# Gated cross-attention with a routed feed-forward layer: four row buffers, W_qv loaded earlier, high halves of the first rows first, the last tile in column halves, and 36 matmuls that nobody reads

## The reference

```
x   = x + tanh(g_xattn) * xattn(layernorm(x), ctx)      # x: 4096 x 512, ctx: 3202 x 512
        Sim     = softmax over ctx of a trilinear similarity;  hq_hat = softmax(Sim) @ ctx
        hc_bar  = softmax(rowmax(Sim)) @ hc               # one row for all
        feats   = [hc, hq_hat, hc * hq_hat, hc * hc_bar];  feats @ W_qv + b_qv      # W_qv: 2048 x 512
x   = x + tanh(g_ffn) * ffn(layernorm(x))
        gates = softmax(x @ w_router);  top 2 of 8 experts, at most 640 rows for each
        h = gelu(rows @ w1[e] + b1[e]);  out = h @ w2[e] + b2[e];  weighted sum for each token
```

## Time and profile before

| | us |
|---|---|
| median of 3 runs | 2236.64 (2236.12 to 2238.46) |
| the profiled execution, its own time | 2254.05 |
| its span, first to last instruction | 2252.3 |
| PE busy in the span | 2172.4 (96%) |
| DVE busy | 1301.3 (58%) |
| ACT busy | 1142.2 (51%) |
| GpSimd busy | 145.7 (6%) |
| mean granted TensorE clock | 0.989 of full speed |

### The profile page before, as it was taken

One profiled execution on the slowest core, in us unless ns is written; L12 is line 12 of the kernel. 1 busy time (PEld: TensorE's weight loads), 2 busy tenths in 40 slices (PEclk: granted clock), 3 DMA queues, 4 the chain that ended last, 5 costly groups with the idle time before them and its releaser, 6 DMA issues.

```text
span 2252.3 us, 34528 instructions
## 1 busy us (share of the span) xinstructions
PE 2172.4 (96%) x12015; PEld 1123.7 (50%) x12015; DVE 1301.3 (58%) x2712; ACT 1142.2 (51%) x1747; POOL 145.7 (6%) x141
## 2 busy tenths in 40 slices
PE   5999999999999999999999995999999999999997
PEld 2444444444444444444455442646565565647463
DVE  7756566655555665554667665555556464646450
ACT  6765565655555655655433342625354363636260
POOL 0000000000000000000022222010101010010101
PEclk9999999999999999999999997999999999999999
DMA  9534444444444444335987762353433333343511
GB/s 250 133 86 94 111 110 104 106 111 93 92 108 109 111 97 115 87 84 120 269 232 206 186 160 50 144 128 100 103 102 98 107 93 107 93 116 117 132 35 23
DMA packets 484566, 265.91 MB, mean 118 GB/s; under 512 B 423860, under 2 KB 423988, under 8 KB 480428
## 3 DMA queue, kind: packets, MB, share of 16 engines
q1 hardware_dynamic: 473644, 244.90, 41.6%
q0 software_dynamic: 10880, 20.52, 4.8%
HBM read 97.96 MB, written 71.52 MB: 75 GB/s over the span
## 4 chain that ended last, share of the span: by engine, by line
PE 88%; DMA 4%; DVE 4%; issue 2%; ACT 1%; POOL 1%; SPq 0%; POOLq 0%; DVEq 0%; ACTq 0%
PE ps L1217 23%; PE ps L1233 22%; PE ps L2012 19%; PE ps L2027 18%; PE ps L1719 5%; DMA rows<-arena 2%; PE ps L367 1%; POOL rows L1426 1%; DMA arena<-arena 1%; DMA arena<-in_ctx 1%; DVE arena L202 0%; DMA feats<-arena 0%; DVE arena L742 0%; DMA arena<-feats 0%; ACT arena L1667 0%
## 5 line engine op out<-in xcount | busy, mean ns | idle before, releaser
L1217 PE MATMUL ps<-arena 128*128 128x512 f16 (+1 forms) x2688 | 557.0, 358 | 4.8 <-DMA arena<-arena 3.1
L1233 PE MATMUL ps<-arena 128*128 128x512 f16 x2400 | 552.9, 379 | 0.0
L2012 PE MATMUL ps<-arena 128*128 128x320 f16 x3072 | 421.1, 300 | 12.2 <-DMA arena<-rows 12.2
L2027 PE MATMUL ps<-arena 128*128 128x512 f16 x1920 | 415.7, 379 | 0.0
L1217 PEld LDWEIGHTS ps<-arena 128*128 128x128 f16 x2688 | 250.1, 98 | 285.5 <-issue 4.9
L1233 PEld LDWEIGHTS ps<-arena 128*128 128x128 f16 x2400 | 233.6, 98 | 275.7
L2012 PEld LDWEIGHTS ps<-arena 128*128 128x128 f16 x3072 | 301.5, 98 | 131.5 <-DMA arena<-rows 12.2
L1038 ACT ACTIVATE arena<-ps,arena 128x512 f32<-128x512 f32 (+1 forms) x224 | 163.4, 731 | 389.6 <-PE ps L1217 389.5
L2027 PEld LDWEIGHTS ps<-arena 128*128 128x128 f16 x1920 | 187.9, 98 | 225.2
L758 DVE TENSOR_REDUCE arena<-arena 128x1 f32<-128x512 f32 (+1 forms) x224 | 139.9, 626 | 192.5 <-ACT arena L1038 191.7
L771 DVE SCALAR_TENSOR_TENSOR arena<-arena 128x512 f16<-128x512 f32 x192 | 144.1, 751 | 182.4 <-ACT arena L1059 182.4
(11 more groups left out here) (245 smaller groups left out, 1380.3 us busy)
## 6 DMA issues: line engine op xcount, KB each, us to landing
arena<-in_L_ffn_w SPq DMA_DIRECT2D x64, 1024.0 KB, 10.2
feats<-arena SPq DMA_DIRECT2D x48, 512.0 KB, 2.8
arena<-in_x SPq DMA_DIRECT2D x32, 512.0 KB, 3.6
rows<-arena SPq DMA_DIRECT2D x13, 774.0 KB, 3.7
out<-arena SPq DMA_DIRECT2D x16, 512.0 KB, 3.0
arena<-in_ctx SPq DMA_DIRECT2D x6, 1024.0 KB, 13.4
arena<-arena SPq DMA_TRANSPOSE x276, 3.1
arena<-in_L_xattn_W_qv SPq DMA_DIRECT2D x4, 1024.0 KB, 7.9
```

The costliest lines, as they stand in the source:

```text
L1217: mm = pe.matmul(out, qT[:, q, s * KD + k, :], ctxT[:, r * KD + k, a:z], start=(k == 0 and s + r == 0), stop=(k == KD - 1 and s == 1))
L1233: mm = pe.matmul(psO[q], turned, ctxN[:, j, r, :], start=(j + s + r == 0), stop=False)
L2012: mm = pe.matmul(psH[:, f % 2, h, :], w1s[:, s, k * F + f * P:k * F + (f + 1) * P], XT[:, r, k, h * HALF:(h + 1) * HALF], start=(k + s + r ...
L2027: mm = pe.matmul(psO[:, t % 2, :], hT[:, f, s, t * P:(t + 1) * P], w2s[:, r, f * D:(f + 1) * D], start=(f + s + r == 0), stop=(f == KF - 1 ...
```

## The change

It has five parts. In the diff `n` counts the steps of W in their new order.

1. **W_qv.** The four parts of W lie in two places of SBUF. Parts 0 and 1 are loaded in `body(NB - 1)` (`load_early`), parts 2 and 3 behind the turns of pieces 1 and 2 of the last body. ACT's `sum_part` 0 and 1 move to pieces 0 and 1 of `half(NB, 0)`, 2 and 3 to pieces 4 and 5. The features and rows of the first merged block are loaded behind the turn of piece 4 (`load_first`), ahead of the turns of pieces 5 and 6, instead of behind them. DVE makes the scales and the first 5 low parts (`AHEAD`) at piece 1 of `half(NB, 1)`, ahead of the fold. W is split and multiplied in the order of parts 1, 2, 0.
2. **Row buffers.** Four by b modulo 4, for all blocks. ACT's high half and the two info words of block b wait for the scatters of block b-4, on the scatters' own semaphores. ACT makes the high half from `x2` with scale and bias, not from `xn`. Bias additions stand ahead of `route_2`, those of the last block within block 14. w1's largest values are taken in blocks 4 to 7, its scales in block 8, its splits in blocks 9 to 12. DVE, ACT and GpSimd have no loops any more in this stage.
3. **The last block.** ACT takes its exponentials ahead of the high half and the square root of the next tile; PE's router and turns stand a few matmuls elsewhere.
4. **36 matmuls** (`keep_running`) that nobody reads stand at the end of PE's stage two. The turns of an expert's rows are four, high and low halves apart, and layer 1 takes both products with the high rows first.
5. **The end.** The last tile of the last expert is made in two column halves; the gate is multiplied into the bias beforehand, so that DVE alone stands between PE and GpSimd.

```diff
         self.W = take([4 * KD, D], F32)
...
+        self.W = [early[:, 0:KD, :], early[:, KD:2 * KD, :], late[:, 0:KD, :], late[:, KD:2 * KD, :]]
+        self.ORDER = tuple(range(KD, FT)) + tuple(range(KD))
...
-                if last and 1 <= c < 5:
+                if last and c in (1, 2):
                     if c == 1:
                         sp.wait_ge(qk_done, NC * U)
-                    mg.load_weights(sp, c - 1)
+                    mg.load_weights(sp, c + 1)
...
                 if c == 4 and not first:
                     store_f(u - 3, 1)
+                if last and c == 4:
+                    load_first()
...
             if last:
-                load_first()
+                load_second()
...
+                if early and c in (1, 3):
+                    load_early(c // 2)
...
+                if last and i and c == 1:
+                    mg.scales(dve)
+                    for n in range(AHEAD):
+                        mg.low(dve, n)
...
-                if last and not i and c >= 4:
-                    mg.sum_part(act, c - 4)
-                if last and i and c == 0:
-                    mg.sum_part(act, 3)
+                if last and not i and c in (0, 1, 4, 5):
+                    mg.sum_part(act, c if c < 2 else c - 2)
...
-    LAST = 5
-    SPLITS = {5: (0, 1), 6: (2, 3), 7: (4, 5), 8: (6, 7)}
+    MAXES = {4: 0, 5: 1, 6: 2, 7: 3}
+    SCALED = 8
+    SPLITS = {9: (0, 1), 10: (2, 3), 11: (4, 5), 12: (6, 7)}
+    NR = 4
+    RUNS = 36
...
+        for b in range(NB - 1):
+            pool.wait_ge(r_step, RK * (b + 1))
+            if b >= 2:
+                pool.wait_ge(sent[(b - 2) % NR], earlier(b - 2) + 16 * 2 * QT)
             for q in range(QT):
-                scatter(v, q, v)
+                scatter(b % NR, q)
...
         def body(b):
+            v, n = b % 2, b // 2
             dve.wait_ge(x_loaded[v], 16 * (n + 1))
+            for q in range(QT):
+                add_bias(b, v, q)
+            if b >= 2:
+                route_2_of(b - 2)
...
+            if b >= NR:
+                act.wait_ge(sent[r], earlier(b))
+            act.wait_ge(y_step, YK * b + YN + 2)
+            for q in range(QT):
+                act.activation(halves[r][:, q, 0:D], x2[v][:, q, :], ACT.Identity, bias=shift[:, q:q + 1],
+                               scale=rs[:, q:q + 1]).then_inc(hi_done, 1)
...
+        sd_last(0)
+        exp_of(NB - 2)
+        high_last(0)
+        copy_turned(NB - 1, 0)
+        exp_last(0)
+        sd_last(1)
+        high_last(1)
...
+        def keep_running():
+
+            for _ in range(RUNS):
+                pe.matmul(psY[1][:, 0, :], ident, Wt[:, 0, 0, :], start=True, stop=True)
...
             for h in range(2):
...
+                for r in range(2):
+                    sp.dma_start_transpose(XT[:, r, :, h * HALF:(h + 1) * HALF],
...
+                    for s, r in ((0, 0), (1, 0), (0, 1)):
+                        if f == 0 and s == 0:
+                            pe.wait_ge(xt_loaded[h][r], 16 * (e + 1))
...
+        for c in range(2):
+            cols = slice(c * D // 2, (c + 1) * D // 2)
+            dve.wait_ge(o_done, ST * E + c)
+            dve.scalar_tensor_tensor(out=oa[TL % 2][:, cols], in0=psL[:, c, :], scalar=ali[:, TL:TL + 1],
+                                     in1=o32[TL % 2][:, cols], op0=ALU.mult, op1=ALU.add).then_inc(o_scaled, 1)
```

More of the change, by code:

```diff
@@ L549, in blank_rows, with load_early, body @@
                 .then_inc(rows_blank, 16)
-        def body(b, first=False, last=False, norms=True, loads=True, piece=None):
+        def load_early(n):
+            if n == 0:
+                for q in range(QT):
+                    sp.wait_ge(q_turned[q], 16 * (NB - 1))
+                sp.wait_ge(row_step, RK * U)
+                sp.wait_ge(e_out, 16 * NB)
+            mg.load_weights(sp, n)
+        def body(b, first=False, last=False, norms=True, loads=True, piece=None, early=False):
             u = 2 * b
@@ L989, in vector @@
             half(NB, i, last=True, norms=False)
-        for k in range(FT):
-            mg.low(dve, k)
+        for n in range(AHEAD, FT):
+            mg.low(dve, n)
         mg.router_scale(dve)
@@ L1172, in scalar @@
             half(NB, i, last=True, norms=False)
-        for k in range(FT):
-            mg.high(act, k, mg.scaled)
-            if k == 2:
+        for n in range(FT):
+            mg.high(act, n)
+            if n == 2:
                 mg.gates(act)
@@ L1464, in norm_part @@
+        def norm_part(b, v):
+            r = b % NR
             s = Steps(dve, y_step, b, YK)
[L1465 removed]
+            s.n = QT + 2 * QT
             s.wait()
[L1467 to L1470 removed]
             for q in range(QT):
@@ L1849, in experts @@
     AK = 7
+    TL = ST - 1
     def sync(sp):
@@ L1887, in add_rows @@
         def add_rows(e, more=True):
-            for t in range(ST):
+            for t in range(ST if more else TL):
                 pool.wait_ge(o_scaled, ST * e + t + 1)
```

407 lines of the change are left out of this document (202 added, 205 removed).

## The result

The changed kernel takes 2230.4 us (median of 7 runs) against 2237.6 us for the kernel before (2236.1 to 2241.3, 7 runs). One of the seven runs of the changed kernel took 13217 us and tells nothing of it; the other six are 2228.4 to 2231.8, their median is 2229.7. The ratio, without that run, is 0.9964, with a 95% interval of 0.9953 to 0.9974. That is 7.2 us less by the medians of seven. Forecast were 20.6 us, and 2230.4 lies above the range of 2208 to 2227.

A forecast was written before the change was run, and what follows sets the result against it. PE was taken as the bound, busy 2172.4 us of a 2252.3 us span. Terms -19.6 + 2.4 + 0.5 - 2.2 - 1.7 = -20.6 us, taken off 2236.6, gave 2216.0 us, range 2208 to 2227.

The forecast's parts named there:

- The step that failed: Final sum: -20.6 us, read from the profiled execution, carried over unchanged to the runs' median of 2236.6, giving 2216.0.
- the stall of the scatters: Stage two: high halves wait for block b-2's scatters, about 7 us late; block 14 would be turned 12.9 us earlier.
- DVE, named as late next: Stage two's split blocks: DVE needs 16.6 of 17.09 us; rival that it becomes the bound: 2224, chance 0.10.
- the one on code without loops: Stage two rival: fetching straight code holds DVE up; at 2 us a block over 15 blocks 2246, chance 0.03.
- the table loads: Last block: by the skill's 1.38 us drain per table switch, parts 2 and 3 would give about 17 us.
- the forecast loss of 2.4: Attention's end: PE waits 5 us for piece 5 and loses clock, so the first merge ends 2.4 us later.
- the term of 1.9 us: First merge: 72 matmuls took 17.4 us behind a 2.9 us wait, against 15.5 at full pace.
- attention's end gains after all: Rival: piece 5 comes in time, 1.6 gained instead of 2.4 lost, no block 2 wait: 2211.5, chance 0.15.
- A wait for block 2's features: Stage two: block 2's features are issued later, giving 0.5 us of new wait (0 to 2).
- part 4's 2.2 us: First expert's layer 1: PE starts at full clock, first row of h 8.5 us behind the issue instead of 10.9.
- The one at 2229: Stage two rival: GpSimd, not the buffers, is late; part 3's own 6.7, parts 4 and 5 remain: 2229, chance 0.03.

The follow-up runs named there:

- after_again: The changed kernel, unchanged, run again on another chip where the kernel before took 2238.0 us: 2229.7 us, ratio 0.9966.
- before_third: The kernel before, unchanged, run once more for its trace on a chip where it took 2238.0 us: 2237.6 us.
- only_attention: The kernel before with only part 1 of the change (attention): 2249.3 us, ratio 0.9998.
- before_again: The kernel before, unchanged, run again on the chip where it took 2250.9 us: 2248.9 us, ratio 0.9991.
- after_no_runs: The changed kernel without the 36 matmuls that nobody reads: 2229.5 us, ratio to the kernel before 0.9966.
- wait_two_route_first: The changed kernel with ACT's high half waiting for block b-2's scatters and route_2 ahead of the bias additions: 2229.4 us, ratio to before 0.9957.
- after_delay_all: The changed kernel with two extra DVE operations ahead of route_2 in every block from 2 on: 2232.6 us, ratio to before 0.9929.
- only_merge: The kernel before with only the changed stage two (parts 2 and 3, the 36 matmuls): 2231.4 us, ratio 0.9919.
- after_wait_two: The changed kernel with ACT's high half waiting for the scatters of block b-2 again: 2251.4 us, ratio to before 1.006.
- before_trip: The kernel before with two extra DVE operations ahead of route_2 in block 8 alone: 2239.4 us, ratio 1.0002.
- only_experts: The kernel before with only the experts' part (quarters of part 4, part 5, without the 36 matmuls): 2248.3 us, ratio 0.9988.
- before_delay_feats: The kernel before with two extra DVE operations ahead of route_2 from block 2 on, features loaded behind the normalization, store first: 2244.5 us, ratio 0.9981.
- before_delay_all: The kernel before with two extra DVE operations ahead of route_2 in every block from 2 on: 2261.0 us, ratio 1.0046.

## Why the prediction was wrong

Where the profiles differ, from milestone to milestone (us, after less before):

| stretch | forecast | profile after less profile before | after_again less before_third |
|---|---|---|---|
| to the first turn of stage two | +2.4 | -2.2 | -3.2 |
| first turn to the issue of the first expert's turns | +0.5 - 19.6 | -19.8 | -6.4 |
| issue to layer 1 (the forecast counts its first matmuls too) | -2.2 | -1.2 | -1.6 |
| layer 1 to the end | -1.7 | -1.8 | -1.1 |
| span | -20.6 | -25.1 | -12.3 |

**The step that failed** is the last one: "It is 17.4 us above the median of the runs, and I cannot place that difference; the sum is carried over as it is". Of the 20.6 us, 12.9 were the stall of the scatters, and the median of the runs does not have that stall. Before_third shows it: block 14 is turned at 1349.03, and the prediction had worked out 1349.5 for the kernel without a stall. The profile of before and before_third differ by 14.5 us of span, and 13.4 of these lie between the first turn and the issue of the first expert's turns: most of the 17.4 us that could not be placed was this very term. The error was to take the stall off a median in which it was not. Without it the same sum is 7.7 us, and 2236.6 less 7.7 is 2228.9, 1.5 us below what was measured. That it comes so near is in part luck: the 7.7 hold a loss of 2.9 us in attention, and the traces without a stall show a gain of 3.2 there and 12.3 in all (last column).

**Part 2.** Mechanism and size were right wherever the stall is: stage two alone gave 19.4 us on the chip of 2250.9. The forecast had named the scatters of block b-2 as 7 us late. That is the longest of the seven waits, which are 2.6 to 7.3; their cost to PE was read rightly from the turns. It did not ask why a landing should take that long at one execution and not at the next. What makes them land late is, for the larger part, the load of the features issued on top of them. DVE, named as late next by a margin of 0.5 us, did not become the bound: turns stay 17.09 us apart in blocks 9 to 12, so that rival is out, and so is the one on code without loops.

**Part 3.** The last block of after, timeline of DVE, its first and last step, against the earlier trace rows:

```profile
1350.44 0.75 DVE L1597 SCALAR_TENSOR_TENSOR arena<-ps,arena 128x512 f32<-128x512 f32 x1 [0.65 <-PE ps L1734]
...
1372.30 0.22 DVE L1567 SCALAR_TENSOR_TENSOR arena<-arena 128x2 f32<-128x2 f32 x1
```

That is 22.1 us, forecast 22.4, and DVE starts 3.1 behind the turn of block 14 where 3.0 were forecast. Between the two kernels without a stall, the stretch shrinks by 6.4, forecast 6.7. On the table loads: the timeline of ACT has a load of 1.28 us and the exponential 0.01 behind its end, as in the earlier trace rows:

```profile
1352.48 1.28 ACT L1675 ACT_TABLE_LOAD   x1
1353.77 0.22 ACT L1675 ACTIVATE arena<-arena 128x20 f32<-128x20 f32 x1
```

By the Trainium skill (ScalarE: Activation LUTs, What ACT_TABLE_LOAD costs) a further drain of about 1.38 us would come with each switch. No row here shows it (this load starts 0.02 us behind the activation ahead of it), so the row was rightly preferred.

**Part 1** was mis-sized, and for most pairs of traces in sign. Forecast was that piece 5 would be issued at about 1080, land at about 1085, and that PE would wait 5 us for it in the products. In after it was issued at 1078.51, landed at 1083.04, and PE waited 0.36. The landing was forecast well; the other end was not. PE came to piece 5 at 1082.7 and not at 1079.6. The prediction had counted 60 matmuls and left out the ten small ones between them (1.0 us in the trace of before), and PE itself ran 1.9 us later, of which 1.3 are a wait for DVE's L828. So the products end at 1086.7 instead of 1091.4. The merge then runs at full pace without a wait, 15.70, as forecast (15.5).

The mechanism that the prediction described is not imaginary. In only_attention PE waited 2.0 us for piece 5 and came back at a lower clock (0.52 from 1084 to 1086), so that 15 matmuls took 5.10 us instead of 3.41:

```profile
1083.42 5.10 PE L1255 MATMUL ps<-arena 128*128 128x512 f16 x15 [2.01 <-DMA arena<-arena]
...
1088.57 15.70 PE L369 MATMUL ps<-arena 128*128 128x512 f16 x72
```

Before_again, from the same chip, starts its merge 2.4 us earlier and has the same pace:

```profile
1086.13 15.70 PE L367 MATMUL ps<-arena 128*128 128x512 f16 x72 [1.89 <-DMA arena<-feats]
```

That is the forecast loss of 2.4, in this one pair. In the executions of before and before_third the merge takes 17.4 and 17.3 at a clock that has fallen, so that the term of 1.9 us is not in every execution either. Over all traces with the attention of before, the first turn of stage two is at 1109.5 to 1112.9 (nine traces, median 1111.4); with the attention of after it is at 1108.5 to 1110.0 in seven and at 1112.0 in only_attention. The rival "attention's end gains after all", at 0.15, was nearer: 1.6 forecast, about 2.2 to the first turn in the profiles. The runs of only_attention show neither (0.9998, 0.9987 to 1.0009). A wait for block 2's features did not come in after; in after_no_runs, wait_two_route_first and after_delay_all it is 0.35 to 0.49, where 0.5 was forecast, but before_again has one of 0.37 as well.

The Trainium skill (DMA: Bandwidth & Descriptors, Queues, rings and completion order) has it that each DMA engine takes the descriptors of a ring in order. Piece 5 took 4.5 us from its issue to its landing behind the features, longer than the 3.1 of the earlier trace rows with nothing in front, so the trace is in line with that.

**Part 4.** Busy time by windows of after: the 36 matmuls and what follows (PE, weight loads, DVE, ACT, POOL, then the granted clock).

```profile
1369.60:1373.00 3.40, 3.40 (x11) 1.25 (x12) 2.55 (x21) 0.00 (x0) 1.01 (x2) 0.51 0.08 18
1373.00:1375.00 2.00, 2.00 (x11) 0.94 (x10) 0.00 (x0) 0.00 (x0) 1.35 (x2) 1.00 0.02 5
1375.00:1379.30 4.30, 4.19 (x20) 1.69 (x18) 0.00 (x0) 0.00 (x0) 0.59 (x1) 1.00 0.29 62
```

The granted clock is 0.51 up to 1373.0 and 1.00 behind it, and all 36 take 9.52 us (10.3 forecast). Layer 1 starts at full clock. In after_no_runs the clock is 0.50 there. But the first 384 matmuls take as long as in the profile of before, and 0.7 us longer than in before_third (54.6 in after_again, 54.0 there). The chain that ended last in after says why:

```profile
1384.59 7.42 DMA arena<-in_L_ffn_w
1392.03 2.29 DVE arena L159
1394.31 0.80 DVE arena L1967
...
1395.30 0.89 ACT arena L2019
...
1396.24 39.30 PE ps L2057 x288
```

From 1380.76 to 1435.53 it is 54.8 us, where the earlier trace rows have 54.83. The clock's gain goes into two waits for the later quarters (0.71 and 0.81), and layer 1 comes to DVE before DVE is free: the load of w2 is issued behind the turns, its largest value (L159) stands ahead of DVE's first part of h. In the traces the 36 matmuls are worth about 1.1 us (54.8 against 55.9 for the 384), in the runs nothing (2229.7 against 2229.5). So of part 4's 2.2 us only the earlier start is left, 1.2 and 1.6 in the two pairs of traces.

**Part 5** came as forecast. Between the last matmul and GpSimd stands one operation of DVE, 0.50 us, and from the last matmul to the end it is 12.0 us instead of 13.9. In the chain, ACT's piece of the earlier trace rows is gone:

```profile
2215.21 0.50 DVE arena L2007
...
2216.50 1.54 POOL out L1930
```

**The rivals.** The one at 2229, that GpSimd and not the buffers is late, came out in its number and not in its mechanism. Its number is that of any case in which there is no stall to remove, and it had 0.03. A rival "the median has no stall" would have had the same sum and belonged there, with the 17.4 us for it.

**What stays open.** Between the two traces without a stall lie 12.3 us, between the medians of the same chip 8.3. After_again's profiled execution is at the lower end of its runs (2227.2 to 2231.7) and before_third's at the upper end of before's (2236.5 to 2240.6), which would account for it; no run tells more. Why before takes 2251 us on some chips and 2238 on others is known down to DVE's late start of `route_1`, but not what holds it there. Whether the meeting delays the scatters on the DMA engines or in the issue was not separated. The changed kernel itself never ran on a chip where before is near 2250: what it gains there, near 20 us, is inferred from only_merge and after_delay_all.

## What to carry to other kernels

When the profiled execution is slower than the median of the runs by more than the noise, look whether the term that you are about to remove is the difference: a stall that exists in one execution and not in another is worth its size only where it exists. Ask of each late landing what was issued at the same moment, since moving that other transfer, or issuing this one about 1 us earlier, may do what a second pair of buffers does. What the extra buffers buy is steadiness: kernels with the changed stage two and its wait four blocks back took 2229 to 2233 us on all chips, while before went from 2238 to 2251.

## What the runs showed of the hardware

- One program, unchanged, took 2238.0, 2239.2, 2248.9 and 2250.9 us on four occasions. Its traces with and without the longer time (before and before_again against before_third) differ mainly by one stall in stage two.
- Scatters that went out on top of a transposing load of 256 rows had landed only 5.4 and 9.1 us after the last one's issue (blocks 8 and 9 above), against a median of 2.7 in before_third from 1230 us on. In one block of after_wait_two the two scatters ahead of that load landed after 2.5 and 4.0 us, the two behind it after 7.6 and 7.4. In the kernel before, 0.70 us of distance between the last scatter and that load was enough to avoid it (before_trip), 0.02 us was not (only_experts). A landing of 5 us alone is no sign of it: in blocks 3 to 6 of before_third the first scatter of a block took 4.5 to 5.1 us with the load 3.7 us behind the last, and nothing waited for it.
- A plain store issued within 0.8 us of the last scatter goes with a late landing too, a smaller one: 4.4 us in the profile of before (store at 1356.20, scatter at 1356.48), and the five waits of 1.5 to 2.7 us in before_delay_feats. No run moved the store alone.
- A stalled scatter sequence shows in its own issue in kernels before: the third of four takes 1.22 to 1.31 us on POOL in the profile of before and in before_delay_all, 0.97 in before_third. In after_wait_two, whose waits are the longest, it stays at 0.97.
- DVE began a step 2.0 us after the matmuls that it waits for in the profile of before (block 6), at once in before_third. Such late starts are in all traces from the two chips on which before took about 2250 us and in none from the two on which it took about 2238.
- How long PE had waited did not alone tell whether the clock fell. Ahead of the same 72 matmuls of the merge, waits of 2.9 us (profile of before) and 3.5 (before_third) were followed by a granted clock of 0.57 and 0.50, and the 72 took 17.4 and 17.3 us. Waits of 3.2 (before_delay_feats) and 3.7 (only_experts) were not: the clock stayed at 1.00 and the 72 took 15.70.
